# Attention's begin in a fused transformer kernel: sign rows by a copy, first stack from the projections, a store moved behind the max rows, fewer maxima in front

## The chip, the cores and the metric

The kernel is one program on 1 core of one Trainium2 chip. The metric is the device time in microseconds (us) of one execution. The times before are 1017.41, 1018.27 and 1013.22 us; the profiled execution is a further one.

## The reference, cut to what matters

Two macaron layers run over x, which has 1024 tokens of width 256. Each layer is half a feed-forward block, a mixing block, and half a feed-forward block again. The mixing block of the first layer is causal attention with 16 heads of width 16, and it is all that the change touches:

```
x = x + 0.5 * moe0(layernorm(x))
Q, K, V = (layernorm(x) @ W.T + b, split in 16 heads of 16)
scores = Q @ K.T / 4, causal mask          # 1024 x 1024 for each head
x = x + softmax(scores) @ V @ Wo.T + bo
x = x + 0.5 * moe0(layernorm(x))
...                                        # second layer: 8 experts, state-space mixer, 8 experts
```

## The kernel before

The kernel runs one queue of instructions on each engine, written out by hand; semaphores order them. PE is the matrix engine, DVE, ACT and POOL are the vector, scalar and GpSimd engines, SP only issues DMA copies. An engine does its instructions strictly in the order of the program.

**Attention's begin.** Behind the layernorm, PE makes eight projection groups (list `PROJ`: for each half e of the 256 output columns the matrix wk, then wq, each in two groups s of 512 tokens; L1241), each of 6 matmuls. ACT reads each group out of its PSUM bank as a rounded fp16 part (L1389), DVE subtracts that from the bank to get the small rest (L1431), so that q and k exist as a high and a low fp16 part. Two banks take turns. Then PE makes eight V tiles (L1251), and DVE adds their bias (L1438).

**Stacks.** The score products of a head want 3 x 16 rows of q and of k one above the other: high and low parts in the order of `ORDER`. SP stores the parts of q and k to DRAM (L1209, `wq_dram`, `wk_dram`, six copies for each half e, counted by `s_pd[e]`), and `stacks` (L1184) loads the 48 rows of a head from there. A pair of heads needs four such copies, q and k for two heads; they land in one of four slots, `qs[slot]` and `ks[slot]`. SP loads pair 0, ACT's queue pairs 1 and 2 and later, inside the loop, pairs 3 to 7.

**Maxima.** The softmax subtracts the row maximum of each query. For each pair, PE makes the scores once more in 12 pieces (`M_PIECES`; L1272, L1278) in two alternating pairs of banks, and DVE takes the maximum of each (L1454). Every fourth piece closes half s = 0 of a pair and every twelfth half s = 1; DVE then turns the columns (L1444) into `mt`. SP's `max_rows` stores `mt[s]` to `max_dram` (L1198), waits for its landing, and loads it as row 48 of `qs` for both heads (L1203). Opposite it in `ks` stands a row of -1 (`MAX_ROW`, written with its neighbours by DVE's memsets, L1425 and L1434), so that the matmul itself subtracts the maximum. The next pair's `mt[s]` waits until the store of this one's landed (`s_ms`).

**The loop.** The pairs' scores run in 8 x 5 = 40 steps g: scores (L1296, L1304), exponentials by ACT (L1408), the product with V (L1324) one step later, and the maxima of later pairs between them. `maxima_at(g)` says which pieces stand at which step: `M_LEAD = 9` steps ahead, so that 22 pieces (12 of pair 0, 10 of pair 1) stand ahead of step 0, and then 12 in each five steps (3, 2, 3, 2, 2, repeated). In front of the maxima PE runs 12 dummy matmuls, and 2 behind each piece (`keep_awake`, L114). The first score of a pair waits for its max rows (`s_mr`).

**Beside it.** `store_w1(2)` and `store_w1(3)` store the second half of a later layer's weights (4 copies of 1024 KB, L2308). They stand in SP's queue between the last store of q and k and the first `max_rows`. DVE waits for them only ahead of the next feed-forward block (`s_rows`). POOL splits other weights in 20 chunks, from the first score on (L1535 to L1548), and DVE's last additions of attention (L1519) wait for the last of these stores.

Of the kernel before, what the change touches and what calls it, by code (L numbers as in the profile page):

```python
# [10 lines left out]
F32 = mybir.dt.float32  # L11
F16 = mybir.dt.float16
# [25 lines left out]
NEG = -1e30  # L38
# [1032 lines left out]


def maxima_at(g):

    out, at = [], 0
    p, i = divmod(g + M_LEAD, NS)
    if 0 <= p < PAIRS:
        at = sum(M_STEPS[:i])
        out = [(p, n) for n in range(at, at + M_STEPS[i])]
    return out  # L1080

# [10 lines left out]
def attention_stage(c, src, A, region, mats, mats_ready, stage, stage_free, before_heads, store_w1):  # L1092
# [15 lines left out]
    w2l = region.take([2, W2_CHUNK], F16)  # L1108
    qs = region.take([STACKS - 1, T], F16)
    ks = region.take([STACKS - 1, T], F16)  # L1110
    spent = Region(region.tensor, region.size + 8 * D * KD)
    spent.at = region.size
    qs, ks = ([x[:, i, :] for i in range(STACKS - 1)] + [spent.take([T], F16)] for x in (qs, ks))
    at = region.at
# [25 lines left out]

    s_c = n("c", 16 * 4)
    s_m = n("m", 2)
    s_pj = n("pj", 8)
# [4 lines left out]
    s_va = n("va", NT)  # L1148
    s_ld = [c.sem(f"tile_in{i}", 16 * 4 * ((PAIRS + STACKS - 1 - i) // STACKS)) for i in range(STACKS)]
    s_sm = n("sm", PAIRS * NM)  # L1150
# [70 lines left out]

# [8 lines left out]
    def pe(eng):  # L1230
        L["pe"](eng)
        eng.wait_ge(*mats_ready)
        for j, (m, e, s) in enumerate(PROJ):
            eng.wait_ge(*L["lo"]((s + 1) * NT // 2 if m == "wk" else NT))
            if j >= 2:
                eng.wait_ge(*s_pl(j - 1))
            wh, wl = mats[m]
            i = 0
            for k in range(KD):
                for w, x in ((wh, c.XTh), (wl, c.XTh), (wh, c.XTl)):  # L1240
                    ins = eng.matmul(c.bank(j % 2), w[:, k, e * P:(e + 1) * P], tokens(m, x, k, s), start=(i == 0), stop=(i == 3 * KD - 1))  # L1241
                    i += 1
            ins.then_inc(s_pj.sem, 1)
        wh, wl = mats["wv"]
        for t in range(NT):
            if t >= 2:
                eng.wait_ge(*s_va(t - 1))
            i = 0
            for k in range(KD):
                for x, w in ((c.XTh, wh), (c.XTh, wl), (c.XTl, wh)):  # L1250
                    ins = eng.matmul(c.bank(2 + t % 2)[:, 0:D], x[:, k, t * P:(t + 1) * P], w[:, k, :],  # L1251
                                     start=(i == 0), stop=(i == 3 * KD - 1))
                    i += 1
            ins.then_inc(s_v.sem, 1)
# [5 lines left out]
        def maxima(p, n):  # L1260
# [3 lines left out]
            if n == 0:  # L1264
                eng.wait_ge(*s_ld[slot](64 * (p // STACKS + 1)))
            if i >= 2:
# [73 lines left out]

        for g in range(-M_LEAD, 0):
            for p, n in maxima_at(g):
                maxima(p, n)
                keep_awake(c, eng, 4, 2)
        for g in range(PAIRS * NS):
# [37 lines left out]
    def act(eng):  # L1383
        L["act"](eng)
        eng.wait_ge(*s_c(64))
        for j, (m, e, s) in enumerate(PROJ):
            eng.wait_ge(*s_pj(j + 1))
            b = 0 if m == "wq" else 1
            eng.activation(qk[m][0][:, e, s * BANK:(s + 1) * BANK], c.bank(j % 2), ACT.Identity, bias=bias[:, b, e:e + 1])\  # L1389
                .then_inc(s_ph.sem, 1)  # L1390

        eng.wait_ge(*s_pd[0](16 * 6))
        eng.wait_ge(*s_m(1))
        for p in range(1, STACKS - 1):
# [16 lines left out]

    def dve(eng):
        L["dve"](eng)
        link = c.dve_link
        eng.wait_ge(*s_c(64))
        eng.memset(zero32[:, :], 0.0)
        eng.memset(mh[:, :, :], 0.0)
        eng.tensor_copy(mask[:, 0:2, :], maskf[:, 0:2, :])
        eng.tensor_scalar(mask[:, 2:4, :], maskf[:, 2:4, :], NEG, None, ALU.mult)
# [7 lines left out]
        for j, (m, e, s) in enumerate(PROJ):  # L1427
            eng.wait_ge(*s_ph(j + 1))
            b = 0 if m == "wq" else 1
            tok = slice(s * BANK, (s + 1) * BANK)  # L1430
            eng.scalar_tensor_tensor(qk[m][1][:, e, tok], c.bank(j % 2), bias[:, b, e:e + 1], qk[m][0][:, e, tok],  # L1431
                                     ALU.add, ALU.subtract).then_inc(s_pl.sem, 1)
        for j in range(2):
            ins = eng.memset(ks[STACKS - 1][64 * j + 32:64 * j + 64, :], -1.0)  # L1434
        ins.then_inc(s_m.sem, 1)
        for t in range(NT):
            eng.wait_ge(*s_v(t + 1))
            eng.tensor_tensor(va[:, t, :, 0:DK], c.bank(2 + t % 2)[:, 0:D].rearrange("p (h v) -> p h v", v=DK),  # L1438
                              bv[:, :].rearrange("p (h v) -> p h v", v=DK), ALU.add).then_inc(s_va.sem, 1)
# [130 lines left out]
def attention_layouts(v):  # L1570
# [892 lines left out]
```

## Time and profile before

| what | before |
|---|---|
| median of three runs (lowest to highest) | 1017.41 us (1013.22 to 1018.27) |
| profiled execution, its own time | 1023.02 us |
| its span, first to last instruction | 1021.4 us |
| mean granted TensorE clock | 0.947 |
| PE, DVE, ACT, POOL busy | 858.3, 585.5, 395.8, 498.3 us |
| attention, first projection to last addition | 160.5 to 356.4 us |

Times in the rows are us from the span's start. A row of the timeline has its start, its length, engine and line, output and input; in square brackets stands how long the engine had been idle before it, and who ended that. "x6" is the number of instructions in the row. A q behind an engine's name (SPq, ACTq) is the engine's issue of a DMA copy. The chain of waits follows the work that ended last backwards, so that its rows are those that set the end.

### The profile page before, as it was taken

How to read it: one execution, taken by the hardware profiler on the slowest of the kernel's cores; microseconds unless marked ns; L12 is line 12 of the kernel's file. 1: busy time of each engine (PE TensorE's matmuls, PEld its weight loads, DVE VectorE, ACT ScalarE, POOL GpSimd, SP SyncE). 2: the span in 40 equal slices, each digit the busy share in tenths (PEclk: the TensorE clock that was granted, in tenths of full speed). 3: DMA queues.
4: the chain of work that ended last, by engine and by line, in shares of the span. 5: the costliest groups of instructions: out<-in, count | busy, mean ns of one | idle time of the engine just before them, and what ended most of it. 6: DMA issues, size and time to landing. Idle time of an engine off the chain costs nothing.

```text
span 1021.4 us, 21582 instructions
## 1 busy us (share of the span) xinstructions
PE 858.3 (84%) x7796; PEld 552.1 (54%) x7797; DVE 585.5 (57%) x1107; ACT 395.8 (39%) x957; POOL 498.3 (49%) x536
## 2 busy tenths in 40 slices
PE   3089986878877789998889999987889978999995
PEld 2046642323322344665578999634334444888994
DVE  5723345678988342334645555676699746544555
ACT  6322223126547442223244444277211152543441
POOL 2316758418888631212244554223988632544531
PEclk9999998999979978999799999999999998999998
DMA  8312654555555317202386665300000003675654
GB/s 295 113 37 93 206 182 139 181 187 180 180 178 158 117 54 290 92 22 69 113 323 230 247 218 207 99 1 1 0 1 1 0 32 136 222 246 180 220 182 140
DMA packets 47817, 142.25 MB, mean 139 GB/s; under 512 B 10641, under 2 KB 23778, under 8 KB 41218
## 3 DMA queue, kind: packets, MB, share of 16 engines
q0 software_dynamic: 19280, 93.40, 27.0%
q1 hardware_dynamic: 22430, 40.92, 11.4%
q10 hardware_dynamic: 6036, 6.95, 2.1%
q8 instruction: 50, 0.82, 0.3%
q14 instruction: 21, 0.17, 0.1%
HBM read 106.11 MB, written 35.16 MB: 138 GB/s over the span
## 4 chain that ended last, share of the span: by engine, by line
PE 56%; DVE 12%; DMA 9%; POOL 8%; issue 7%; ACT 7%; SPq 1%; another core or an unknown queue 0%; ACTq 0%; DVEq 0%; POOLq 0%
PE psum L570 15%; PE psum L543 10%; PE psum L529 10%; PE psum L1324 3%; DMA mem<-xn_dram,mem 2%; POOL mem L2133 2%; PE psum L114 2%; POOL mem L2129 2%; DMA wq_dram<-mem 2%; PE psum L554 2%; DMA max_dram<-mem 1%; PE psum L1296 1%; PE psum L516 1%; PE psum L1272 1%; DVE mem L1454 1%
## 5 line engine op out<-in xcount | busy, mean ns | idle before, releaser
L570 PE MATMUL psum<-mem 128*128 x1536 | 181.7, 274 | 7.1 <-issue 3.0
L570 PEld LDWEIGHTS psum<-mem 128*128 128x128 f16 x1536 | 146.3, 98 | 30.6 <-issue 11.3
L919 POOL DMA_INDIRECT y_dram<-mem x64 | 64.1, 1001 | 162.0 <-DVE mem L826 159.5
L661 ACT ACTIVATE mem<-psum,mem 128x128 f32<-128x128 f32 x368 | 104.7, 373 | 82.6 <-PE psum L543 42.9
L543 PE MATMUL psum<-mem 128*128 128x128 f16 x2208 | 132.3, 219 | 0.4 <-issue 0.2
L543 PEld LDWEIGHTS psum<-mem 128*128 128x128 f16 x2208 | 127.2, 98 | 2.1 <-issue 1.0
L914 POOL DMA_INDIRECT mem<-xn_dram,mem x64 | 67.0, 1048 | 108.1 <-PE psum L516 81.1
L1408 ACT ACTIVATE mem<-psum 128x512 f32<-128x512 f32 (+1 forms) x160 | 79.9, 552 | 76.3 <-PE psum L1304 53.3
L529 PE MATMUL psum<-mem 128*128 x432 | 103.0, 398 | 1.6 <-issue 1.6
L114 PE MATMUL psum<-ones 128*128 128x512 f16 x324 | 100.4, 435 | 0.6 <-issue 0.6
L1454 DVE TENSOR_REDUCE mem<-psum 128x2 f32<-128x1024 f32 (+2 forms) x96 | 87.8, 949 | 17.8 <-PE psum L1278 8.7
L817 DVE CAST mem<-mem 128x512 f16<-128x512 f32 x92 | 41.1, 446 | 98.3 <-ACT mem L661 89.7
L805 DVE TENSOR_TENSOR mem<-mem,psum 128x1024 f32<-128x1024 f32 x18 | 22.0, 1222 | 95.8 <-ACT mem L652 95.8
L529 PEld LDWEIGHTS psum<-mem 128*128 128x128 f16 x432 | 44.0, 102 | 54.2 <-issue 11.4
L895 POOL DMA_INDIRECT mem<-w_rows,mem x46 | 50.1, 1090 | 45.9 <-issue 24.7
L648 ACT ACTIVATE mem<-psum 128x256 f16<-128x256 f32 x64 | 24.8, 387 | 107.0 <-PE psum L516 104.8
L819 DVE TENSOR_TENSOR mem<-mem 128x512 f16<-128x512 f32 x92 | 64.3, 698 | 3.2
L1840 PE MATMUL psum<-mem 128*128 128x512 f32 x112 | 54.1, 607 | 10.9 <-DVE psum L2055 10.6
L196 PE MATMUL psum<-ident,mem 128*128 128x128 f32 x96 | 24.3, 341 | 35.1 <-ACT mem L180 35.0
L652 ACT ACTIVATE mem<-psum 128x1024 f32<-128x1024 f32 x18 | 18.4, 1024 | 88.4 <-PE psum L529 88.4
L516 PE MATMUL psum<-ident,mem 128*128 128x128 f32 x128 | 25.7, 284 | 31.2 <-DVE mem L315 14.1
L1324 PE MATMUL psum<-mem 128*17 128x384 f32 (+3 forms) x480 | 50.2, 453 | 0.7
(251 smaller groups left out, 1476.0 us busy)
## 6 DMA issues: line engine op xcount, KB each, us to landing
stage<-in_w POOLq DMA_DIRECT2D x20, 480.0 KB
stage<-in_w POOLq DMA_DIRECT2D x16, 512.0 KB
w_rows<-mem SPq DMA_DIRECT2D x8, 1024.0 KB, 8.4
w2h_dram<-mem POOLq DMA_DIRECT2D x20, 240.0 KB, 2.9
w2l_dram<-mem POOLq DMA_DIRECT2D x20, 240.0 KB, 3.4
xn_dram<-mem ACTq DMA_DIRECT2D x32, 128.0 KB, 1.7
mem<-w2h_dram SPq DMA_DIRECT2D x2, 2048.0 KB
mem<-w2l_dram SPq DMA_DIRECT2D x2, 2048.0 KB
```

The source lines that it names most:

```text
L114: eng.matmul(c.bank(bank), c.ones16[:, :], wide, start=True, stop=True)
L529: ins = eng.matmul(c.bank(2 * m + s), a[:, p, k, :], w[:, at], start=(i == 0), stop=(i == 3 * KD - 1))
L543: ins = eng.matmul(c.bank(2 * p + j // half)[:, j % half * P:(j % half + 1) * P], mats[q][:, l, k, j * P:(j + 1) * P], x[:, p, k, :], star ...
L570: ins = eng.matmul(c.bank(6)[:, 0:D], a[:, 0 if gated else p, q * half + j, :], w[:, at], start=(i == 0), stop=(i == 3 * CF - 1))
L661: ins = eng.activation(h[:, p, j * P:(j + 1) * P], c.banks(2 * p, 2)[:, j * P:(j + 1) * P], ACT.Gelu, bias=slabs[s][:, KD * FF + j:KD * FF ...
L819: eng.tensor_tensor(hTl[:, p, part, :], gelu, hTh[:, p, part, :], ALU.subtract).then_inc(s_hl.sem, 1)
L914: eng.indirect_dma_start(xg[:, b % 2, :], None, c.xn_dram[:, :], bass.IndirectOffsetOnAxis(ap=idx[:, b:b + 1], axis=0)).then_inc(s_xg[b % ...
L919: eng.indirect_dma_start(c.y_dram[:, :], bass.IndirectOffsetOnAxis(ap=yidx[:, b:b + 1], axis=0), yo[:, b % 2, :], None).then_inc(s_ys[b % ...
L1324: ins = eng.matmul(c.bank(7)[at:at + VW, a - y * BANK:a - y * BANK + w], va[:, k, 2 * p + j, :], pt[:, g % RING, 2 * y + j, off:off + w], ...
L1408: eng.activation(pt[:, g % RING, 2 * y + j, 0:w], c.bank(4 + at % 3)[:, 0:w], ACT.Exp, scale=DK ** -0.5).then_inc(s_ex.sem, 1)
L1454: eng.tensor_reduce(out, c.banks(2 * (i % 2), 2).rearrange("p (j q) -> p j q", j=2)[:, :, 0:w], AX.X, ALU.max)\
L1840: ins = eng.matmul(acc(2 * p + j), gm[:, i % RING, j, :], xw[:, i % RING, j, :], start=False, stop=True, skip_group_check=True)
```

## The change

- The row of -1 now comes by DMA from a constant in DRAM (`guard_rows`, `minus_ones`): two copies for slots 0 to 2 behind the other constants (the wait `s_c` of ACT, DVE and POOL includes them), two for slot 3 behind the stores of q and k. DVE's eight memsets go.
- Pair 0's stack no longer takes the way through DRAM: `first_stack` copies 16 rows at a time from the projections' SBUF tiles, 12 copies, nine issued by SP ahead of the stores, three by ACT ahead of its sixth group.
- The projections use four banks in turn, V's tiles banks 4 and 5.
- `store_w1(2)` and `store_w1(3)` stand behind the last `max_rows`.
- 16 pieces of maxima instead of 22 stand ahead of step 0 (`M_BEGIN`); each of steps 0 to 5 takes one more, from step 6 on all is as before.
- The wait for the mask and for all projections moves with these.

```diff
+M_BEGIN = 16
...
+def pieces_until(g):
+
+    if g < 0:
+        return M_BEGIN
+    p, i = divmod(g + M_LEAD, NS)
+    steady = NM * p + sum(M_STEPS[:i + 1]) if p < PAIRS else NM * PAIRS
+    ramp = M_BEGIN + sum(M_STEPS[(x + M_LEAD) % NS] + 1 for x in range(g + 1))
+    return min(steady, ramp)
...
 def maxima_at(g):
...
+    return [divmod(i, NM) for i in range(pieces_until(g - 1) if g >= 0 else 0, pieces_until(g))]
...
+    def first_stack(eng, m, j):
+
+        dst = (qs if m == "wq" else ks)[0]
+        for g, part_ in enumerate(ORDER[m]):
+            eng.dma_start(dst[64 * j + DK * g:64 * j + DK * (g + 1), :], qk[m][part_][j * DK:(j + 1) * DK, 0, :]).then_inc(s_ld[0].sem, 16)
+
+    def guard_rows(eng, i):
+
+        for j in range(2):
+            row = 64 * j + MAX_ROW
+            eng.dma_start(ks32[i][row:row + 1, :], A["minus_ones"][0:1, 0:ks32[i].shape[1]]).then_inc(s_c.sem, 16)
...
+        guard_rows(eng, 0)
...
+        eng.wait_ge(*s_pl(2))
+        for j in range(2):
+            first_stack(eng, "wk", j)
+        eng.wait_ge(*s_pl(4))
+        first_stack(eng, "wq", 0)
         for e in range(KD):
...
-            if e == 0:
-                eng.wait_ge(*s_pd[0](16 * 6))
-                eng.wait_ge(*s_m(1))
-                stacks(eng, 0)
+        guard_rows(eng, 1)
         eng.wait_ge(*s_pd[1](16 * 6))
-        store_w1(eng, 2)
-        store_w1(eng, 3)
         for p in range(PAIRS):
             for s in range(2):
                 max_rows(p, s)
+        store_w1(eng, 2)
+        store_w1(eng, 3)
...
-            if j >= 2:
-                eng.wait_ge(*s_pl(j - 1))
+            if j >= 4:
+                eng.wait_ge(*s_pl(j - 3))
...
+                if p == STACKS - 1:
+                    eng.wait_ge(*s_c(16 * 8))
...
-        eng.wait_ge(*s_c(64))
+        eng.wait_ge(*s_c(96))
         for j, (m, e, s) in enumerate(PROJ):
+            if j == 5:
+                eng.wait_ge(*s_pl(4))
+                first_stack(eng, "wq", 1)
             eng.wait_ge(*s_pj(j + 1))
...
-        for i in range(STACKS - 1):
-            for j in range(2):
-                ins = eng.memset(ks[i][64 * j + 32:64 * j + 64, :], -1.0)
-        ins.then_inc(s_m.sem, 1)
```

SP's queue from the projections to the first max rows, in the kernel before (`att_pl` counts DVE's rests of the projections, `att_pd1` the second half's stores, `att_mt` DVE's turned maxima):

```order
L1209 DMA wq_dram<-mem 128x1024 [waits att_pl]
L1209 DMA wq_dram<-mem 128x1024 x2
L1184 DMA mem<-wq_dram 48x1x1024 [waits att_m,att_pd0]
L1184 DMA mem<-wq_dram 48x1x1024
L1184 DMA mem<-wk_dram 48x1x1024 x2
...
L2308 DMA w_rows<-mem 128x2x1024 [waits split_lo,att_pd1]
L2308 DMA w_rows<-mem 128x2x1024
L2308 DMA w_rows<-mem 128x2x1024 [waits split_lo]
L2308 DMA w_rows<-mem 128x2x1024
L1198 DMA max_dram<-mem 4x32x32 [waits att_mt]
L1203 DMA mem<-max_dram 1x2x256 [waits att_ms0]
```

The same place of SP's queue in the changed kernel, from the constants on:

```order
L1211 DMA mem<-in_minus_ones 1x1536 x2
L1205 DMA mem<-mem 16x1024 [waits att_pl]
L1205 DMA mem<-mem 16x1024 x5
L1205 DMA mem<-mem 16x1024 [waits att_pl]
L1205 DMA mem<-mem 16x1024 x2
...
L1242 DMA wq_dram<-mem 128x1024 [waits att_pl]
L1242 DMA wq_dram<-mem 128x1024 x2
L1211 DMA mem<-in_minus_ones 1x512 x2
L1226 DMA max_dram<-mem 4x32x32 [waits att_mt,att_pd1]
L1231 DMA mem<-max_dram 1x2x256 [waits att_ms0]
L1231 DMA mem<-max_dram 1x2x256
```

The nine 16-row copies stand ahead of the twelve stores, the 48-row loads of pair 0 are gone from between them, and the first store of maxima has no weights' store in front.

DVE's queue from the constants to the first maxima, in the kernel before:

```order
L1422 MEMSET psum 128x512
L1425 MEMSET mem 32x1024 x6
L1431 SCALAR_TENSOR_TENSOR mem<-psum,mem 128x512 x8
L1434 MEMSET mem 32x1024 x2
L1438 TENSOR_TENSOR mem<-psum,mem 128x16x16 x8
L1454 TENSOR_REDUCE mem<-psum 128x2 x4
```

The same place in the changed kernel:

```order
L1454 MEMSET psum 128x512
L1455 CAST mem<-mem 128x256
L1456 TENSOR_SCALAR mem<-mem 128x256
L1461 SCALAR_TENSOR_TENSOR mem<-psum,mem 128x512 x8
L1465 TENSOR_TENSOR mem<-psum,mem 128x16x16 x8
L1481 TENSOR_REDUCE mem<-psum 128x2 x4
```

Six memsets in front of the first projection's rest and two in front of V's additions are gone; the two mask instructions, which stood ahead of the PSUM memset, now stand behind it.

## Rows read from the trace of the kernel before

**Rows 1.** Windows: us; PE, PEld, DVE, ACT, POOL busy; PEclk; DMA share; GB/s

```profile
162.00:170.00 8.00, 1.24 (x6) 0.39 (x4) 6.30 (x10) 1.37 (x2) 7.53 (x6) 0.91 0.45 132
182.00:205.00 23.00, 18.89 (x133) 8.93 (x130) 14.66 (x23) 1.97 (x2) 9.03 (x11) 0.93 0.46 173
205.00:222.00 17.00, 11.94 (x85) 3.54 (x84) 11.36 (x16) 0.25 (x1) 0.00 (x0) 0.90 0.51 195
222.00:240.00 18.00, 14.99 (x214) 6.00 (x214) 15.48 (x20) 14.07 (x28) 13.81 (x13) 1.00 0.54 166
```

**Rows 2.** Chain of waits, start and us: copies that set the end

```profile
178.19 3.27 DMA wq_dram<-mem
...
187.91 13.64 DMA wq_dram<-mem
...
204.93 9.91 DMA max_dram<-mem
...
275.58 5.24 DMA max_dram<-mem
...
281.43 5.83 DMA mem<-max_dram
```

**Rows 3.** Timeline of DVE, 163 to 215 us

```profile
163.15 0.91 DVE L1425 MEMSET mem<- 32x1024 f16 x1 [0.25 <-issue]
...
182.77 0.75 DVE L1431 SCALAR_TENSOR_TENSOR mem<-psum,mem 128x512 f16<-128x512 f32 x1 [1.06 <-ACT mem L1389]
...
195.42 0.43 DVE L1454 TENSOR_REDUCE mem<-psum 128x2 f16<-128x256 f32 x1 [3.14 <-PE psum L1278]
...
207.28 0.17 DVE L1461 TENSOR_TENSOR mem<-mem 128x8 f16<-128x8 f32 x1
...
214.94 0.21 DVE L1444 STREAM_TRANSPOSE mem<-mem 128x32 f16<-128x32 f16 x1 [4.15 <-DMA max_dram<-mem]
```

**Rows 4.** Timeline of PE, 160 to 222 us

```profile
160.48 0.59 PE L1241 MATMUL psum<-XTh,mem 128*128 128x512 f16 x2
...
170.80 1.01 PE L1241 MATMUL psum<-XTh,mem 128*128 128x512 f16 x2 [7.57 <-DVE mem L1431]
...
186.38 0.61 PE L1251 MATMUL psum<-mem,XTh 128*128 128x256 f16 x2 [3.05 <-DVE mem L1438]
...
192.38 2.75 PE L114 MATMUL psum<-ones 128*128 128x512 f16 x12 [0.56 <-issue]
...
221.24 0.39 PE L1296 MATMUL psum<-mem 49*128 49x512 f16 x2
```

**Rows 5.** Timeline of ACT: last projection, first copies of pair 2

```profile
182.05 0.69 ACT L1389 ACTIVATE mem<-psum,mem 128x512 f16<-128x512 f32 x1 [1.13 <-PE psum L1241]
...
185.61 1.41 ACTq L1184 DMA_DIRECT2D mem<-wq_dram  x2
```

**Rows 6.** Timeline of SP's issues, 201 to 220 us

```profile
201.57 3.31 SPq L2308 DMA_DIRECT2D w_rows<-mem  x4
...
216.11 0.56 SPq L1198 DMA_DIRECT2D max_dram<-mem  x1
218.08 1.15 SPq L1203 DMA_DIRECT2D mem<-max_dram  x2
```

**Rows 7.** Windows, same columns: the copies' tail, and the weights' store

```profile
199.00:200.00 1.00, 1.00 (x10) 0.29 (x8) 0.97 (x3) 0.00 (x0) 0.00 (x0) 1.00 0.20 78
207.00:210.00 3.00, 2.81 (x27) 1.00 (x26) 2.92 (x7) 0.00 (x0) 0.00 (x0) 1.00 1.03 408
```

**Rows 8.** Page, part 5: the maxima's reductions

```profile
L1454 DVE TENSOR_REDUCE mem<-psum 128x2 f32<-128x1024 f32 (+2 forms) x96 | 87.8, 949 | 17.8 <-PE psum L1278 8.7
```

**Rows 9.** Timelines of SP, POOL and DVE: attention's last rows

```profile
330.54 1.14 SPq L1203 DMA_DIRECT2D mem<-max_dram  x2
...
349.04 0.54 POOL L1548 DMA_DIRECT2D w2l_dram<-mem  x1
...
353.68 2.75 DVE L1519 TENSOR_TENSOR X<-psum,X 128x256 f32<-128x256 f32 x8 [0.64 <-PE psum L1337]
```

More of the change, by code:

```diff
@@ L1070, in unit_width @@
     return sum(query_span(k, y)[1] for k in S_KEYS[y][i])
-def maxima_at(g):
[L1075 to L1080, printed above, removed]
+def pieces_until(g):
[5 more added lines that the diff above has]
+    return min(steady, ramp)
+def maxima_at(g):
+    return [divmod(i, NM) for i in range(pieces_until(g - 1) if g >= 0 else 0, pieces_until(g))]
 def attention_weights(c, A, region):
@@ L1109, in attention_stage @@
     qs = region.take([STACKS - 1, T], F16)
+    at = region.at
+    ks32 = [region.take([(STACKS - 1) * T // 2], F32)]
+    region.at = at
     ks = region.take([STACKS - 1, T], F16)
@@ L1112, in attention_stage @@
     spent.at = region.size
-    qs, ks = ([x[:, i, :] for i in range(STACKS - 1)] + [spent.take([T], F16)] for x in (qs, ks))
+    qs = [qs[:, i, :] for i in range(STACKS - 1)] + [spent.take([T], F16)]
+    at = spent.at
+    ks32.append(spent.take([T // 2], F32))
+    spent.at = at
+    ks = [ks[:, i, :] for i in range(STACKS - 1)] + [spent.take([T], F16)]
     at = region.at
@@ L1139, in attention_stage @@
     CL = c.XTl[:, :, :].rearrange("p k t -> p (k t)").rearrange("p (g q) -> p g q", q=BANK)
-    s_c = n("c", 16 * 4)
-    s_m = n("m", 2)
+    s_c = n("c", 16 * 8)
+    s_m = n("m", 1)
     s_pj = n("pj", 8)
@@ L1148, in attention_stage @@
     s_va = n("va", NT)
-    s_ld = [c.sem(f"tile_in{i}", 16 * 4 * ((PAIRS + STACKS - 1 - i) // STACKS)) for i in range(STACKS)]
+    s_ld = [c.sem(f"tile_in{i}", 16 * 4 * ((PAIRS + STACKS - 1 - i) // STACKS) + (16 * 8 if i == 0 else 0)) for i in range(STACKS)]
+    stack_count = lambda p: 64 * (p // STACKS + 1) + (16 * 8 if p % STACKS == 0 else 0)
     s_sm = n("sm", PAIRS * NM)
@@ L1240, in pe @@
                 for w, x in ((wh, c.XTh), (wl, c.XTh), (wh, c.XTl)):
-                    ins = eng.matmul(c.bank(j % 2), w[:, k, e * P:(e + 1) * P], tokens(m, x, k, s), start=(i == 0), stop=(i == 3 * KD - 1))
+                    ins = eng.matmul(c.bank(j % 4), w[:, k, e * P:(e + 1) * P], tokens(m, x, k, s), start=(i == 0), stop=(i == 3 * KD - 1))
                     i += 1
@@ L1250, in pe @@
                 for x, w in ((c.XTh, wh), (c.XTh, wl), (c.XTl, wh)):
-                    ins = eng.matmul(c.bank(2 + t % 2)[:, 0:D], x[:, k, t * P:(t + 1) * P], w[:, k, :],
+                    ins = eng.matmul(c.bank(4 + t % 2)[:, 0:D], x[:, k, t * P:(t + 1) * P], w[:, k, :],
                                      start=(i == 0), stop=(i == 3 * KD - 1))
@@ L1264, in maxima @@
             if n == 0:
-                eng.wait_ge(*s_ld[slot](64 * (p // STACKS + 1)))
+                eng.wait_ge(*s_ld[slot](stack_count(p)))
             if i >= 2:
@@ L1339, in project @@
             return ins
[L1341 to L1344, printed above, removed]
+        for p, n in maxima_at(-1):
+            maxima(p, n)
+            keep_awake(c, eng, 4, 2)
         for g in range(PAIRS * NS):
@@ L1384, in act @@
         L["act"](eng)
-        eng.wait_ge(*s_c(64))
+        eng.wait_ge(*s_c(96))
         for j, (m, e, s) in enumerate(PROJ):
+            if j == 5:
+                eng.wait_ge(*s_pl(4))
+                first_stack(eng, "wq", 1)
             eng.wait_ge(*s_pj(j + 1))
             b = 0 if m == "wq" else 1
-            eng.activation(qk[m][0][:, e, s * BANK:(s + 1) * BANK], c.bank(j % 2), ACT.Identity, bias=bias[:, b, e:e + 1])\
+            eng.activation(qk[m][0][:, e, s * BANK:(s + 1) * BANK], c.bank(j % 4), ACT.Identity, bias=bias[:, b, e:e + 1])\
                 .then_inc(s_ph.sem, 1)
         eng.wait_ge(*s_pd[0](16 * 6))
-        eng.wait_ge(*s_m(1))
         for p in range(1, STACKS - 1):
@@ L1414, in dve @@
         link = c.dve_link
-        eng.wait_ge(*s_c(64))
+        eng.wait_ge(*s_c(96))
         eng.memset(zero32[:, :], 0.0)
         eng.memset(mh[:, :, :], 0.0)
-        eng.tensor_copy(mask[:, 0:2, :], maskf[:, 0:2, :])
-        eng.tensor_scalar(mask[:, 2:4, :], maskf[:, 2:4, :], NEG, None, ALU.mult)
         eng.memset(va[:, :, :, DK], 1.0)
@@ L1422, in dve @@
         eng.memset(c.bank(7), 0.0)
-        for i in range(STACKS - 1):
-            for j in range(2):
-                ins = eng.memset(ks[i][64 * j + 32:64 * j + 64, :], -1.0)
-        ins.then_inc(s_m.sem, 1)
-        for j, (m, e, s) in enumerate(PROJ):
-            eng.wait_ge(*s_ph(j + 1))
+        eng.tensor_copy(mask[:, 0:2, :], maskf[:, 0:2, :])
+        eng.tensor_scalar(mask[:, 2:4, :], maskf[:, 2:4, :], NEG, None, ALU.mult).then_inc(s_m.sem, 1)
+        for n, (m, e, s) in enumerate(PROJ):
+            eng.wait_ge(*s_ph(n + 1))
             b = 0 if m == "wq" else 1
             tok = slice(s * BANK, (s + 1) * BANK)
-            eng.scalar_tensor_tensor(qk[m][1][:, e, tok], c.bank(j % 2), bias[:, b, e:e + 1], qk[m][0][:, e, tok],
+            eng.scalar_tensor_tensor(qk[m][1][:, e, tok], c.bank(n % 4), bias[:, b, e:e + 1], qk[m][0][:, e, tok],
                                      ALU.add, ALU.subtract).then_inc(s_pl.sem, 1)
-        for j in range(2):
-            ins = eng.memset(ks[STACKS - 1][64 * j + 32:64 * j + 64, :], -1.0)
-        ins.then_inc(s_m.sem, 1)
         for t in range(NT):
             eng.wait_ge(*s_v(t + 1))
-            eng.tensor_tensor(va[:, t, :, 0:DK], c.bank(2 + t % 2)[:, 0:D].rearrange("p (h v) -> p h v", v=DK),
+            eng.tensor_tensor(va[:, t, :, 0:DK], c.bank(4 + t % 2)[:, 0:D].rearrange("p (h v) -> p h v", v=DK),
                               bv[:, :].rearrange("p (h v) -> p h v", v=DK), ALU.add).then_inc(s_va.sem, 1)
@@ L1490, in turn_back @@
                 eng.tensor_tensor(CL[:, g, :], cx[:, :], CH[:, g, :], ALU.subtract).then_inc(s_cl.sem, 1)
-        for g in range(-M_LEAD, 0):
-            for q, n in maxima_at(g):
-                maxima(q, n)
+        for q, n in maxima_at(-1):
+            maxima(q, n)
         for g in range(PAIRS * NS):
@@ L1524, in pool @@
         before_heads(eng)
-        eng.wait_ge(*s_c(64))
+        eng.wait_ge(*s_c(96))
         eng.wait_ge(*L["xn"](NT))
@@ L1584, in attention_layouts @@
     early = (m < 64) | (m - 64 < j)
+    d["minus_ones"] = np.full((1, 3 * T // 2), 0xBC00BC00, np.uint32).view(np.float32)
     d["causal"] = np.concatenate([m == j, m == j + 64, keys, early], 1).astype(np.float32)
```

2 lines of the change are left out of this document (1 added, 1 removed).

## The prediction, made before the changed kernel ran

> **What bounds the kernel now.** I read attention's begin first in the windows [rows 1]. Between 162 and 170 us PE is busy 1.24 of 8 us; between 205 and 222 it is busy 11.94 of 17 us, much of that with dummy matmuls, while ACT does next to nothing (0.25) and POOL nothing. From 222 on DVE is busy 15.48 of 18 us. So the begin is a chain of waits, and the loop behind it is nearly full on DVE. Then the timelines say what the chain is.
>
> PE starts the projections at 160.48 and stands still for 7.57 us, until DVE has done six memsets of 0.91 us and can free a bank [rows 3, 4]. DVE ends the last projection's rest at 182.77 + 0.75 = 183.5; two more memsets stand ahead of V's additions, and PE waits 3.05 us for those. At 192.38 the 12 dummies start, and DVE's first maximum comes at 195.42. Twelve maxima later, at 207.28 + 0.42 = 207.7, both halves of pair 0 are turned.
>
> SP is not ready for them. Its last store of the projections was issued at 187.91 and landed after 13.64 us, at 201.6 [rows 2]. In the tail of that landing the DMA engines show a share of 0.20 at 78 GB/s [rows 7]: about three of 16 engines work, and these carry the 48-row loads. Then SP issues 4 MB of weights (3.31 us, [rows 6]), which move at 408 GB/s, and the first store of maxima behind them takes 9.91 us, where the next one is landed and read from after 218.08 - 216.11 = 1.97 us. DVE meanwhile waits 4.15 us for the same landing. The first scores come at 221.24 [rows 4]. Everything behind them in attention is counted from there.
>
> **Memsets and banks.** The six memsets cost DVE 6 x (0.91 + 0.25) = 7.0 us ahead of its first rest. The mask instructions moved there are two short ones, and the two constant rows add two issues to SP; I allow 1 us for both, and take nothing: with four banks PE first looks for a rest at its fifth group, over 5 us after its start. So PE runs through. Twelve matmuls of 512 columns take 2.75 us at full clock [rows 4], so 48 take 11.0 and end at 160.5 + 11.0 = 171.5. ACT's extra work is three issues ahead of group six; one pair of its issues took 1.41 us [rows 5], so three take 2.1. The fourth rest is done at 160.5 + 5.5 + 0.69 + 0.75 = 167.4, ACT issues until 169.6 and has two groups to catch up, which it does at 0.69 each by 171.7. The last rest ends at 171.5 + 0.69 + 0.75 = 173.0, in place of 183.5.
>
> **V and first maxima.** From the last rest to the dummies it took 192.38 - 183.5 = 8.9 us. Two memsets with their gaps (2.3) go. PE's clock had fallen in the 3.05 us of idle time, and the two tiles after it took 188.91 - 186.38 = 2.5 us where tiles at full clock take 0.65 each; the new idle time is about 1 us, so 1.2 us more go. 173.0 + 5.4 = 178.4; the dummies and the first piece take the 195.42 - 192.38 = 3.0 us that they took. First maximum at 181.4, which is 14.0 us earlier.
>
> **Pair 0's stack.** It must be there at 181.1. SP can issue its first copy at 160.5 + 2.8 + 1.4 = 164.7 and nine by 171 at up to 0.7 each; some 8 us are left behind the last one, so this is hidden if 16 rows move as a store does. What that is, no row shows. From above, the nearest row is the 48-row load: 96 KB by three engines [rows 7], 25 GB/s for each. Were a 16-row copy on a single engine, 12 x 32 KB would take 15.5 us from 165.5 on, and with that engine's part of the stores (6 x 16 KB, 3.9 us) end at 181 to 185. From below: spread over all engines it is under 1 us each. I take the lower one: the 48 rows are read as three blocks of 16 in DRAM and three engines work, so the outer count, not the rows, seems to set the number; a 16-row copy has no outer count but its rows. The Trainium skill says the same (DMA: Bandwidth & Descriptors, Queues, rings and completion order): a copy uses the largest number up to 16 that divides the slowest dimension on both sides, so 3 for the load and 16 for the copy. By that rule the sum has nothing here, by one engine up to 4 us; the trace agrees on the 3. The same rule speaks against the next step, for the store of maxima has 4 as slowest dimension and shares its engines with the loads of pairs 1 and 2.
>
> **Projections' stores and max rows.** SP issues the twelve stores behind its nine copies, from 171 to 177, the last one after 173.0. The first six land some 3.3 us after the last of them [rows 2], at 177 or 178, and ACT then issues eight loads of 96 KB. At 78 GB/s these keep their engines for 10 us; the second six stores' share there is 3.9 us more. All have landed by 192 at the latest, probably 184 for the stores. The maxima of pair 0 are turned at 181.4 + 12.3 = 193.7. So the stores aren't the last wait any more; at worst the first half's store starts at 192 and delays the second by 1 us. From 193.7 on: store 1.97, two loads' issues 1.15 [rows 6], and their landing, which took at most 221.24 - 219.23 = 2.0. First scores at 198.8, **22.4 us earlier**. PE has its 16 pieces done at about 181.4 + 15.4 = 197 and waits some 2 us. Pair 1's stack is issued first of the eight and wanted at 194; it is there.
>
> **Fewer maxima in front.** Six reductions of 949 ns [rows 8] come into steps 0 to 5, 5.7 us on the engine that was busy 15.48 of 18 us [rows 1]. The gaps that it had, 2.5 us, can hide some. Between 3 and 5.7, I take 5: PE's pieces wait for DVE one by one, so few gaps close. Counted on DVE alone it comes out near: 14.0 earlier at the first maximum, 4.15 of wait and 1.4 of slow clock behind it gone, 3.5 of new wait at the first score, 16.1. By the scores it is 22.4 - 5 = 17.4. I take **17**.
>
> **The store behind.** The last max rows are read at 330.54 + 1.14 = 331.7 [rows 9], now 314.7. 4 MB alone take 10 us at 408 GB/s [rows 7]; beside POOL's chunks (166 GB/s, [rows 1]) some 16, so it lands by 331 to 334. DVE wants it at 356.4 - 17 = 339. POOL's chunks start with the first score and ended at 349.6, 127 us later; now at 326 or, slowed by the store, 330, and attention's last addition wants them at 336.7. Both are hidden by 5 us. The 2 constant rows of slot 3 are hidden by three pairs of steps.
>
> **Rivals.** (1) *The sixteen-row copies are slow*, by one engine as above, or the second stores' landing is later than 192. First maxima up to 4 us later, first scores 3 to 5 later: gain 12 to 14. (2) *The ramp costs more*: pair 1's maxima are complete in step 2 and wanted in step 5, three steps after, where it was five. At the worst seen round trip, 5.24 + 1.15 + 5.83 = 12.2 us [rows 2, 6], that is late by about 2 us beyond 10 us of steps; with DVE's 5.7 the gain is 22.4 - 8 = 14, together with (1) 10. (3) *No change*: the front was not what set the end of attention, POOL's 20 chunks were: they ended at 349.6, just 4 us before the last addition. Against it: they start with the first score, so they move too. Only if the weights' store stretched them by more than the 7 us that they now have, and by 12 more, nothing would be left. (4) *Slower*: the weights' store behind the max rows holds up the next block. It decides when it lands after 356, that is 41 us after its issue, at under 100 GB/s. Rows 7 show four times that, but no row shows it beside the loop's end. At 80 GB/s it would land at 367 and the kernel take 1028 us.
>
> **How the numbers follow.** The profiled execution took 1023.0 us, 5.6 above the median of 1017.4. The sum makes 1006.0 of the first, and **1000.4** of the median. The forecast with its own bounds, 14 to 22 less (all of the six maxima hidden at the one end), has a chance of 0.77; rivals 1 and 2, 8 to 14 less, 0.15; rival 3, within 0.5%, 0.05; rival 4, 0.03. What this kernel can tell from no change is about 0.5%, or 5 us. Range: 1017.4 - 22 = 995 less 1 for the spread of runs, and 1017.4 - 10 = 1007.4: 994 to 1007.5. Faster 0.92, same 0.05, slower 0.03.
>
> **What would show it.** Right: PE's projections without a gap and at full clock, the last rest near 173, first maximum near 181, first scores near 199, their max rows as the last wait; DVE's share up between 199 and 220; last addition near 337 with PE as its releaser. Wrong: an idle PE for the first piece with the 16-row copies as releaser (rival 1); a wait of the scores at step 5 (rival 2); a wait of DVE between attention's last addition and the next layernorm (rival 4); the last addition released by POOL's stores (rival 3). The step most open is what the six maxima cost.

## The result, and the profile after

The changed kernel takes 1007.69 us (median of 20 runs), the kernel before 1017.54 (20 runs): ratio 0.9903, 95% interval 0.9885 to 0.9921. It is faster by 9.85 us, where 17 were predicted; the time lies just outside the range of 994 to 1007.5.

The profiled execution of the changed kernel took 1007.78 us, its span is 1005.9. Its windows, from the first score to 211 us, from there to pair 0's context, and from there to pair 1's (columns as in [rows 1], to be held against the last row there):

```profile
199.14:211.00 11.86, 10.26 (x70) 3.12 (x72) 6.61 (x7) 5.43 (x10) 7.11 (x8) 0.50 0.40 130
211.00:223.91 12.91, 9.84 (x144) 4.04 (x140) 11.39 (x14) 6.31 (x14) 11.63 (x11) 0.97 0.61 185
223.91:244.06 20.15, 15.82 (x190) 5.91 (x192) 16.77 (x20) 10.23 (x21) 17.56 (x17) 0.83 0.59 182
```

PE runs at half clock for the first 12 us of the loop, and pair 0's context (its product with V, turned by DVE) comes 24.8 us after the first score. In the kernel before that took 15.8 (237.0 - 221.24). What lies ahead of the loop came as forecast. The timeline of DVE:

```profile
162.25 0.75 DVE L1461 SCALAR_TENSOR_TENSOR mem<-psum,mem 128x512 f16<-128x512 f32 x1 [0.63 <-ACT mem L1423]
...
171.25 0.75 DVE L1461 SCALAR_TENSOR_TENSOR mem<-psum,mem 128x512 f16<-128x512 f32 x1 [0.17 <-ACT mem L1423]
...
180.18 0.43 DVE L1481 TENSOR_REDUCE mem<-psum 128x2 f16<-128x256 f32 x1 [3.14 <-PE psum L1308]
...
192.05 0.27 DVE L1488 TENSOR_TENSOR mem<-mem 128x8 f16<-128x8 f32 x1
...
223.91 0.71 DVE L1500 STREAM_TRANSPOSE mem<-psum 128x512 f32<-128x512 f32 x1
```

The last rest ends at 172.0 (173.0 predicted, 183.5 before), the first maximum comes at 180.2 (181.4; 195.4 before), both halves of pair 0 are turned at 192.6 (193.7; 207.7 before) [rows 3]. The timeline of PE:

```profile
159.97 0.59 PE L1271 MATMUL psum<-XTh,mem 128*128 128x512 f16 x2
...
172.40 0.39 PE L1281 MATMUL psum<-mem,XTh 128*128 128x256 f16 x2 [0.59 <-DVE mem L1465]
...
177.14 2.75 PE L114 MATMUL psum<-ones 128*128 128x512 f16 x12 [0.56 <-issue]
...
199.14 0.61 PE L1328 MATMUL psum<-mem 49*128 49x512 f16 x2 [4.30 <-DMA mem<-max_dram]
...
208.02 0.61 PE L1302 MATMUL psum<-mem 48*128 48x512 f16 x2 [0.84 <-DVE mem L1481]
...
221.61 0.39 PE L1328 MATMUL psum<-mem 49*128 49x512 f16 x2 [0.47 <-DMA mem<-max_dram]
```

The projections run through, the idle time of 7.57 us is gone and that of 3.05 is 0.59 [rows 4]; the first scores come at 199.1 (198.8 predicted). But behind the 4.30 us of idle time ahead of them the clock is half, and at 221.61 step 5 waits for max rows again, 0.47 us. SP's issues:

```profile
164.26 5.63 SPq L1205 DMA_DIRECT2D mem<-mem  x9
169.94 1.58 SPq L1242 DMA_DIRECT2D wk_dram<-mem  x3
...
186.01 0.62 SPq L1226 DMA_DIRECT2D max_dram<-mem  x1
193.53 1.20 SPq L1231 DMA_DIRECT2D mem<-max_dram  x2
194.76 0.56 SPq L1226 DMA_DIRECT2D max_dram<-mem  x1
...
214.62 0.54 SPq L1226 DMA_DIRECT2D max_dram<-mem  x1
217.46 1.13 SPq L1231 DMA_DIRECT2D mem<-max_dram  x2
```

The nine 16-row copies are issued by 169.9, and no wait names them. Pair 1's second half is turned only at 214.6 and its rows are wanted at step 5: the chain of waits, from there on.

```profile
186.01 7.50 DMA max_dram<-mem
...
194.76 2.03 DMA max_dram<-mem
...
214.62 2.82 DMA max_dram<-mem
...
218.05 3.51 DMA mem<-max_dram
...
221.61 0.39 PE psum L1328 x2
```

In this pair of profiles attention ends only 5.2 us earlier (356.4 to 351.3). A second pair, e17 and e18 below, shows 10.2 us (360.6 to 350.4), and no gain in what lies behind attention.

### The profile page after: what moved, and what is told of

It reads as the page before. It is cut to its first block, busy times and chain, and to the rows that moved or that the text cites. A ratio compares the mean times of both kernels' runs of the same rounds, so it can differ in the third digit from the quotient of the medians.

```text
span 1005.9 us, 21558 instructions
## 1 busy us (share of the span) xinstructions
PE 856.9 (85%) x7784; PEld 553.7 (55%) x7785; DVE 591.5 (59%) x1099; ACT 398.4 (40%) x957; POOL 490.9 (49%) x536
## 4 chain that ended last, share of the span: by engine, by line
PE 61%; DVE 11%; DMA 7%; ACT 7%; POOL 7%; issue 6%; SPq 1%; ACTq 0%; DVEq 0%; POOLq 0%
PE psum L570 16%; PE psum L543 12%; PE psum L529 10%; PE psum L1356 3%; PE psum L114 2%; POOL mem L2160 2%; DMA max_dram<-mem 2%; DVE mem L1481 2%; PE psum L554 2%; PE psum L516 2%; POOL mem L2156 1%; PE psum L1328 1%; ACT mem L180 1%; PE psum L1923 1%; DVE mem L315 1%
## 5 line engine op out<-in xcount | busy, mean ns | idle before, releaser
L570 PE MATMUL psum<-mem 128*128 x1536 | 178.8, 273 | 3.7 <-DVE mem L810 2.5
L529 PE MATMUL psum<-mem 128*128 x432 | 99.3, 388 | 1.6 <-issue 1.6
L817 DVE CAST mem<-mem 128x512 f16<-128x512 f32 x92 | 45.0, 489 | 78.1 <-ACT mem L661 77.0
L895 POOL DMA_INDIRECT mem<-w_rows,mem x46 | 45.4, 986 | 44.9 <-issue 27.1
L1356 PE MATMUL psum<-mem 128*17 128x384 f32 (+3 forms) x480 | 54.3, 490 | 0.5
```

Of the source, the lines that this page charges most:

```text
L529: ins = eng.matmul(c.bank(2 * m + s), a[:, p, k, :], w[:, at], start=(i == 0), stop=(i == 3 * KD - 1))
L570: ins = eng.matmul(c.bank(6)[:, 0:D], a[:, 0 if gated else p, q * half + j, :], w[:, at], start=(i == 0), stop=(i == 3 * CF - 1))
L1356: ins = eng.matmul(c.bank(7)[at:at + VW, a - y * BANK:a - y * BANK + w], va[:, k, 2 * p + j, :], pt[:, g % RING, 2 * y + j, off:off + w], ...
```

## The experiments

Four to a chip, except the last two. A ratio is to the kernel before on the same chip, with its 95% interval. Each profile is of one execution. "Pair 0" is the time from the first score to the first context turned (row 128x512 of DVE, L1473 before, L1500 after).

**e1, 16 dummies over the wait; e2, 22 maxima in front.**

```diff
# e1, behind the loop over maxima_at(-1)
+        keep_awake(c, eng, 4, 16)
# e2
-M_BEGIN = 16
+M_BEGIN = 22
```

> The changed kernel with 16 more dummy matmuls (about 3.6 us) behind the 16 maxima in front, over the wait for the first max rows; nothing else. Theory A (the idle 4.3 us before the first scores drop PE's clock, and the ramp, which has no dummies, then runs some 13 us at half clock): first scores stay at 199, the granted clock of the first pair's steps rises from 0.75 to over 0.95, and the first pair's steps take 20 us or less in place of 24.8; ratio to before about 0.986. Theory B (the five more maxima on DVE are the whole cost): the clock rises but the first pair's steps stay at 24 us; ratio stays 0.990.

> The changed kernel with 22 maxima in front, as before the change (M_BEGIN = 22), all other edits kept. Theory A and the lead: six more pieces with their dummies fill the wait, first scores at 201 to 203, the first pair's steps take 16 us as in the kernel before, pair 1's max rows are no longer waited for at step 5; ratio 0.983 to 0.986. Rival (fewer maxima in front is a gain, as the scores start earlier): slower than the changed kernel, ratio 0.992.

e1: 999.93 us, 0.982 (0.9774 to 0.9865). e2: 997.79 us, 0.980 (0.9758 to 0.9842). In the profile of e1, the slowest of its six runs, 1.44 us of idle time are left and the clock falls all the same: pair 0 took 24.5 us. In e2 the first scores come at 201.6 without any wait and pair 0 takes 15.8 us, as before the change. Fewer maxima in front were no gain but a loss. e2's end shows what the weights' store does there, in the timeline of DVE:

```profile
337.13 2.74 DVE L1545 TENSOR_TENSOR X<-psum,X 128x256 f32<-128x256 f32 x8 [2.09 <-DMA w2l_dram<-mem]
```

The last additions wait 2.1 us for POOL's last store. In its repetition e15 the same row waits 0.64 us, for PE.

**e3, weights' store back in front; e4, behind the max rows of pair 1.**

```diff
# e3: ahead of the loop over p; e4: in it, if p == 1
+        store_w1(eng, 2)
+        store_w1(eng, 3)
```

> The changed kernel with the 4 MB weights' store back ahead of the first max rows. If the store's place is worth what the sum says, the first scores come 8 to 10 us later (at 207 to 209) and the ratio is 0.996 to 1.000. Rival (the store behind costs at the end what it gives in front, since the last pair's steps took 1.6 us longer and the loop is bound by DVE): first scores later, but the ratio stays within 0.002 of 0.990.

> The changed kernel with the weights' store behind the max rows of pair 1 in place of behind the last ones. If the store behind slows the last pairs (the last pair took 16.1 us for 14.4), this gives back about 1.5 us at the end but costs the max rows of pair 2, whose lead of five steps should hide it: ratio 0.988 to 0.990. If the end's 1.6 us are only PE's clock, no difference: 0.990.

e3: 1015.05 us, 0.9984 (0.9946 to 1.0022), first scores at 212.9 behind 16.5 us of idle PE. The store's place is worth 14 us at the first score and nearly the whole gain. e4: 1019.05 us, 1.0026 (1.0 to 1.0052), my figure of 0.988 to 0.990 missed. The chain of waits of e4:

```profile
223.74 20.88 DMA max_dram<-mem
```

One max store takes 20.9 us to land behind the 4 MB in its queue, beyond the lead of a pair: pair 1's steps took 30 us.

**e5, 19 in front; e6, a busy PE in the ramp; e7, pair 0's stack through DRAM; e8, the store issued by ACT.**

```diff
# e5
+M_BEGIN = 19
# e6: 20 dummies behind the front, and in maxima, ahead of the piece
+            if 16 <= i < 36:
+                keep_awake(c, eng, 2 * (i % 2), 2)
# e7 (M_BEGIN = 22): no first_stack; in sync, behind the stores of e == 0
+                eng.wait_ge(*s_pd[0](16 * 6))
+                stacks(eng, 0)
# e8 (M_BEGIN = 22): in act, none in sync
+            if g in (24, 31):
+                store_w1(eng, 2 if g == 24 else 3)
```

> The changed kernel with 19 maxima in front (M_BEGIN = 19), between its 16 and the 22 that gave 0.980. Theory A (what counts is that PE is kept busy over the wait for the first max rows, and that pair 1's maxima end early enough): PE has its pieces done at about the time the max rows land (199.5), no idle time there, and most of the gain is there: ratio 0.981 to 0.984. Theory B (each piece that stays in the steps costs its 0.95 us on DVE and more by what waits on it, whatever the clock): half way, 0.985.

> The changed kernel (16 maxima in front) with 20 dummy matmuls over the wait for the first max rows and two dummies ahead of each of the next 20 pieces of maxima, in the bank that the piece then overwrites; no arithmetic of the kernel is changed. Theory A (the granted clock in the first pairs' steps is the loss): clock of the first pair's steps over 0.9, its 24.8 us fall to 20, ratio 0.980 to 0.983, as 0.4 us of dummies per piece partly replace what the clock gives. Theory B (DVE's five more pieces and the pair 1 max rows' lead): the clock rises, the first pair's steps stay at 23 us or more, ratio 0.987 or above.

> The kernel with 22 maxima in front (0.980), and pair 0's stack again loaded from DRAM behind the first half's stores, in place of the twelve 16-row copies. The sum gave the 16-row copies no cost and their gain only as cover: the stack landed at 181.5 + before; with the projections 10 us earlier it would land at about 182 to 183, some 3 us after the dummies end at 179.8, and the second half's stores and the first max rows come later by the 5 us of the four loads on three engines. Expected first scores at 204 to 206 in place of 201.6, ratio 0.983 to 0.985. Rival (the way through DRAM is hidden behind V's products): 0.980.

> The kernel with 22 maxima in front (0.980), and the weights' store issued by ACT's queue in two halves, ahead of its exponentials of steps 24 and 31, in place of by SP behind the last max rows. With 22 in front the last additions waited 2.1 us for POOL's last store and the block behind them for more, as the 4 MB ran at 382 GB/s beside POOL's last chunks. If that contention is the wait, it goes: attention ends 2 to 3 us earlier, ratio 0.977. Rival (the halves slow the max rows of the last pairs instead, as the store in the middle of SP's queue did with 20.9 us): 0.980 or above.

On this chip the runs spread widely (before: 1021 to 1036). e5: 1012.91 us, 0.983 (0.9774 to 0.9885). That is in theory A's range, but the interval holds B's 0.985 too, and the profile, of the slowest of its six runs, does not look as A said: 1.74 us of idle time are left, the clock falls to 0.50 from 203 on, and pair 0 takes 21.4 us. So it does not decide.

e6: 1019.39 us, 0.9932 (0.9896 to 0.9969): its clock is 1.00, and pair 0 takes 26.3 us. By the letter that is theory B, but the dummies are up to 0.44 us per piece on a PE that is now busy 25.1 of these 26.3 us, DVE 17.2. It takes the clock out and puts as much in, so it separates nothing.

e7: 1024.35 us, 0.9925 (0.9884 to 0.9966): the timeline of PE.

```profile
191.06 0.29 PE L1300 MATMUL psum<-mem 48*128 48x128 f16 x2 [10.03 <-DMA mem<-wk_dram]
```

Ten us of wait for the stack, where I had put 3; the direct copies are worth 12 us at the first score (213.8 against 201.6).

e8: 1012.4 us, 0.9841 (0.9788 to 0.9895): no wait for POOL at the end, but 4.1 us for max rows in the last pairs, as the rival said.

**e9, 24 dummies; e10, the store in four pieces; e11, 22 with the store in front; e12, short reductions.**

```diff
# e9
+        keep_awake(c, eng, 4, 24)
# e10 (M_BEGIN = 22): in max_rows' loop, one copy a pair
+            if p >= PAIRS - 4:
+                store_w1(eng, 2 + (p - PAIRS + 4) // 2, (p - PAIRS + 4) % 2)
# e12: the reduction's columns
+[:, :, 0:w if i < 16 or i >= 33 else 64]
```

> The changed kernel (16 maxima in front) with 24 dummies (5.3 us) over the wait for the first max rows, so that no idle time is left ahead of the first scores; none in the steps. With 16 dummies 1.4 us of idle time was left, and in its profile the clock still fell to half at 201. Theory A (idle time ahead of and in the first steps drops the clock, which costs about 5 us there): clock of the first pair's steps 0.95 or more, its 24.8 us fall to 19 to 20, ratio 0.980 to 0.983. Rival C (the short waits inside the first steps drop the clock whatever comes before): the clock falls again at 202, steps 24 us, ratio 0.985 to 0.990.

> 22 maxima in front, and the weights' store cut in its four copies of 1 MB, one in SP's queue behind the max rows of each of pairs 4 to 7. Each holds up the next max rows by 1 MB, 2.5 us alone and about 5 beside POOL's chunks (4 MB took 20.9). The lead of the max rows is a pair, 17 us, and their trip 11: if that holds, no score waits, and the end's wait for POOL's last store (2 to 3 us) goes: 3 us less than with 22 in front and the store behind. Rival: the trip grows beyond the lead as with ACT's issue (4.1 us of wait for max rows), no gain or a loss of 2 to 4 us.

> 22 maxima in front, and the weights' store back ahead of the first max rows: sign rows by copy, four banks and the direct stack alone against the kernel before. With 16 in front that was 0.998, with 16.5 us of idle PE ahead of the first scores at 212.9. With 22 in front the scores come no earlier (212 to 213), but six pieces are done in that wait: 5 to 6 us less than with 16, ratio 0.992. Rival (DVE's wait for the landing of the first store of maxima blocks these six): 0.998.

> The changed kernel, but the maxima that stand in steps 0 to 5 are taken over only 64 columns per head, so that part of the maximum is left out; DVE's time for these 17 falls from about 16 to 5 us. Theory B (the first pair's steps are bound by DVE's five more maxima): the steps take 17 us or less, ratio 0.982 or below. Theory A (PE at half clock is the bound there, DVE waits for it 13 of 25 us): the steps keep 22 us or more, ratio 0.987 to 0.990.

e9: 1008.23 us, 0.9823 (0.9785 to 0.9861). e12, whose kernel leaves out part of the maximum, is no version to use: 1007.22 us, 0.9807 (0.9761 to 0.9852). Both split what I had held for one cause. The windows of e9 (clock kept) and then of e12 (DVE freed), up to pair 0's context:

```profile
199.77:216.00 16.23, 12.51 (x181) 5.12 (x180) 13.46 (x18) 9.65 (x20) 11.60 (x12) 1.00 0.45 147
216.00:223.41 7.41, 3.75 (x34) 1.10 (x32) 3.32 (x4) 1.88 (x5) 6.51 (x7) 0.84 0.60 191
```

```profile
199.39:211.00 11.61, 11.04 (x104) 3.95 (x106) 2.85 (x11) 6.15 (x12) 6.59 (x8) 0.60 0.36 122
211.00:223.68 12.68, 8.86 (x112) 3.08 (x110) 3.31 (x12) 5.40 (x12) 11.40 (x11) 0.81 0.59 186
```

With full clock up to 216 or with an almost free DVE, the context comes at 223.4 and 223.7, as in the changed kernel. In both the score of step 5 waits over 3 us; the timeline of PE in e9:

```profile
220.50 0.39 PE L1328 MATMUL psum<-mem 49*128 49x512 f16 x2 [3.33 <-DMA mem<-max_dram]
```

Pair 1's second half is turned at 210.0, its store lands after 6.0 us, the second load is issued 0.6 us later and lands after 3.8: a trip of 10.5 us. That was rival 2 of the prediction. The gain of both over the changed kernel comes later: pairs 1 to 4 take 71 us in each in place of 75, and from pair 4's context to attention's end it is 46.9 and 47.0 us in place of 52.1. Attention ends at 341.3 and 341.7, ten us before the changed kernel.

e10: 1008.94 us, 0.9838 (0.9788 to 0.9889), waits of 2.0 us for max rows and 1.2 for a stack in the later pairs, no gain over the store behind. e11: 1014.58 us, 0.9878 (0.9828 to 0.9927), with first scores at 214.4; my 0.992 lies in the interval, the rival's 0.998 does not.

**e13, POOL's chunks later; e14, the changed kernel; e15, e2 again; e16, memsets and two banks.**

```diff
# e13, with e9's dummies, in pool
-        eng.wait_ge(*s_st(1))
+        eng.wait_ge(*s_st(4 * NS + 1))
# e16 (M_BEGIN = 22), c.bank(j % 2), and in dve ahead of the first rest
+        for i in range(STACKS - 1):
+            for j in range(2):
+                eng.memset(ks[i][64 * j + 32:64 * j + 64, :], -1.0)
```

> The changed kernel with the 24 dummies over the wait (as e9), and POOL's chunks begun with step 5's first score in place of step 0's, so that pair 1's max rows travel without them. Theory L (pair 1's max rows, turned 10 us after the first score, take a 10.5 us trip because POOL's chunks share the DMA engines, and step 5 waits for them): the trip from the turned maxima to the score falls to 5 to 7 us, no wait at step 5, pair 0's context is turned 19 to 20 us after the first score in place of 23.6. Rival (the trip is long by the loads of pair 3 on ACT's queue alone): the trip stays at 9 to 10 us, and so does the wait. The total says nothing here, as POOL's chunks then end some 15 us after attention's last product.

> The changed kernel as it is, on the same chip as the next run. The interval of 0.9885 to 0.9921 should hold it: 0.990. First scores at 199, pair 0's context 23 to 25 us later, with half clock or with a wait at step 5.

> The kernel with 22 maxima in front once more, beside the changed kernel on one chip. If its 0.980 was no accident of that chip: 0.978 to 0.983, and 7 to 10 us below the changed kernel. If the difference was the chip's: within 3 us of it.

> 22 maxima in front, and the memsets of slots 0 to 2 back ahead of the first rest, with two banks in turn in place of four; all other edits kept. The sum's term for memsets and banks was 10.5 us at the last rest. Expected: last rest near 182 in place of 172, first scores at 209 to 212 in place of 201.6, ratio 0.988 to 0.991. Rival (the copies of the stack and of the projections were the longer way to the first scores, so memsets cost less): first scores at 206 or earlier, ratio 0.984.

e13, one execution: 1008.04 us. The rows of pair 1 are turned at 209.7 and the score at 216.70 waits for nothing; the context comes at 219.0, 19.5 us after the first score. SP's issues in e13, to be held against those above:

```profile
209.72 0.54 SPq L1226 DMA_DIRECT2D max_dram<-mem  x1
213.16 1.13 SPq L1231 DMA_DIRECT2D mem<-max_dram  x2
```

The store is back after 3.4 us in place of 6.0.

e14: 1005.97 us, 0.9872 (0.9828 to 0.9916). e15: 996.33 us, 0.9813 (0.9783 to 0.9843): 9.6 us below it on one chip, attention's end at 340.2 against 349.1. But e15 is e2's kernel, and its pair 0 took 17.3 us where e2's took 15.8. Its windows, up to pair 0's context and to pair 1's:

```profile
200.56:217.89 17.33, 15.41 (x201) 5.96 (x202) 13.31 (x17) 11.96 (x24) 12.39 (x13) 0.90 0.47 155
217.89:232.87 14.98, 12.63 (x184) 5.00 (x182) 13.43 (x20) 9.99 (x21) 13.17 (x12) 1.00 0.64 200
```

The clock fell to 0.67 between 206 and 209 although nothing waited ahead of the first score, so one execution's clock is no constant of a kernel.

e16: 1005.79 us, 0.9893 (0.9864 to 0.9923): last rest at 184.7, first scores at 213.2. The memsets and banks are worth 12 us there (201.6 in e2, 200.6 in e15).

**e17, the kernel before; e18, the changed kernel,** each as it is, one round.

> The kernel before, as it is, for a second profile beside one of the changed kernel on the same chip. In the first profiles attention ended 5.2 us earlier (356.3 against 351.2), but the spans differed by 15.5, so that 10 us lay behind attention, where no instruction was changed, while the medians differ by 9.85. If that was chance of one execution: attention ends near 356, and from there to the end of the span it takes 655 to 660 us in place of 665. If what lies behind attention gains by the change (the weights' store or POOL's chunks elsewhere): 665 again, and 10 more than in the run beside it.

> The changed kernel on the same chip as the run before this one. From attention's end to the end of the span 654 to 656 us, as in its two profiles so far (654.7, 654.8); attention's end at 349 to 351, if the kernel before has 356 on this chip.

e17: 1014.27 us (one of its eight runs took 1706 us, for no reason that the record shows), 0.9964 (0.9936 to 0.9992) against the same kernel, so that a difference of 0.4% in one round means nothing. e18: 1002.93 us, 0.9866 (0.9729 to 1.0004). Attention ends at 360.6 and 350.4; from there to the span's end it is 655.4 and 656.1. The first profile of before had 665 there, which this one does not repeat.

## Why the prediction was wrong

**The front was right.** Memsets and banks: last rest 11.5 us earlier, 10.5 predicted; e16 puts them at 12. V and first maximum: 15.2 earlier, 14.0 predicted. Pair 0's stack cost nothing, and e7 shows what it saved. By the rule of the Trainium skill (DMA: Bandwidth & Descriptors, Why a DMA increments its semaphore by 16 and not by 1) a 16-row copy works on 16 engines; the trace agrees in so far as twelve copies were there in time, their spread itself is in no row. Projections' stores: max rows of pair 0 started at 186.0 and not at 192; but their store took 7.50 us beside the loads of pairs 1 and 2 (DMA share 0.20 at 74 GB/s from 186 to 193.5), so the second half began 2.2 us after it was turned, where 1 was priced; the first maximum's head start paid for it. First scores 22.1 us earlier in the first profiles, 22.4 predicted, and 24.9 in e17 and e18.

**The step that failed is "Fewer maxima in front".** I took 5 us of 3 to 5.7, counting only six reductions on DVE. The first pair's steps alone grew by 9.0 us (24.8 against 15.8; 25.1 against 15.8 in e18 and e17), and on one chip 16 pieces in front (e14) cost 9.6 us against 22 (e15) in the kernel's time. The runs divide the 9.0 us: 3.8 us are the five pieces themselves (e13: 19.5 us with clock and rows in order). 4.1 us more come from pair 1's max rows (e9: 23.6). With half clock in place of that it is 1.1 more (24.8). Clock and rows overlap: in the changed kernel the maxima are turned at 214.6 in place of 210, and the trip then takes 7 us in place of 10.5, the store 2.8 us in place of 6.0. Of the 4.6 us later 1.3 are in DVE's small maximum of 128x8 (L1488) just before: it takes 1.46 us in place of 0.17, and ends with POOL's instruction beside it (214.35 and 214.33). The rest goes with the half clock. Either way the score of step 5 comes at 220 or 221.6. Rival 2 had this mechanism, at 2 us; I put the steps between at 10 us and the trip at 12.2, but even in e13 only 7.0 us lie between the turned rows and step 5's score, as the rows are turned 10 us after the first score.

**The clock was no term at all.** I saw the wait of 2 us coming (it was 4.30, as PE had its pieces done at 194.8) and gave it no price by the clock. In the kernel before, the pieces behind the 4.62 us of idle time ahead of 216.32 carried two dummies each. Windows of the kernel before:

```profile
216.00:219.00 3.00, 2.68 (x12) 0.65 (x12) 2.40 (x4) 0.00 (x0) 0.00 (x0) 0.55 0.06 9
219.00:222.00 3.00, 2.93 (x21) 0.79 (x20) 2.19 (x4) 0.25 (x1) 0.00 (x0) 0.88 0.03 3
```

The clock was back at 1.00 from 222 on [rows 1]. Now the loop's own steps follow the idle time, and they have no dummies. It stays half for 12 us. That the dummies make this difference is argued: no run has them in the steps alone. Behind that, pair 1's steps have a clock of 0.83 and take 20.2 us, before 0.90 and 17.9. Pairs 1 to 4 took 75.2 us in place of 71.4: about 4 us of loss behind the ramp, which nothing in the prediction foresaw. A full clock in the ramp (e9) or a shorter DVE there (e12) each bring 71 back. The clock within these pairs is not what differs: its mean is 0.86 in the changed kernel, 0.87 in e9 and 0.88 before, and e9's pair 1 takes 17.6 us at 0.78. What the ramp leaves behind that costs these 4 us stays open.

**The store behind** was right in front, where e3 and e11 show 13 to 14 us at the first score. From pair 4's context to attention's end the changed kernel takes 52.1 us in place of 48.0 (50.9 against 49.0 in e18 and e17). The record does not lay that on the store. 2.5 us of the 4.1 are pair 5's steps (299.13 to 317.66), and SP issues the store only at 325.3. Windows of the changed kernel and of e9:

```profile
299.13:317.66 18.53, 15.18 (x184) 5.79 (x182) 14.67 (x20) 10.00 (x21) 16.04 (x16) 0.82 0.52 161
```

```profile
294.47:309.37 14.90, 12.63 (x184) 5.04 (x182) 13.35 (x20) 10.00 (x21) 12.82 (x11) 1.00 0.49 158
```

The other 1.6 are the last pair, 16.1 us at a clock of 0.89 for 14.5 at 1.00, which the kernel before shows too (e17: 15.9 at 0.89). e9 and e12 have the same store behind and take 46.9 and 47.0 us; e3 has it in front and takes 49.8. So this loss goes with the clock; why that is lower there stays open. What the store does cost at the end shows with 22 in front: POOL's last load took 10.1 us in e2, and the last additions waited 2.1 us. Sum for the second pair of profiles: 24.9 - 9.4 - 3.4 - 1.9 = 10.2, which is the measured gain of attention; for the first pair it is 22.1 - 9.0 - 3.8 - 4.1 = 5.2.

**How many maxima stand in front** therefore decides about half of it: with 22 the same edits give 20.5 and 18.0 us (0.9813 and 0.980), about twice the changed kernel's. But the number itself is not the only way: e1 and e9 keep 16 in front, only fill the wait with dummies, and stand at 0.982 with overlapping intervals, although e9's first pair still takes 23.6 us. So most of what e9 wins back (10 us at attention's end) does not come from the first pair's steps.

## What to carry to other kernels

Work that fills a wait is free only while the wait is there, and it may also be what keeps PE's clock up and a later transfer in time; before moving it out, look at what then stands behind the idle time, and price the steps after it too. Count a lead in microseconds from the instruction that completes the data to the one that wants it, with the worst trip seen, and not in steps. A large store ahead of small urgent copies in one queue holds them all up (14 us at the first score here); behind them it was cheap, and in the middle no better than in front (1.003 and 0.998).

## What the runs showed of the hardware

- After 4.30 us of idle PE the granted clock was 0.50 for 12 us, though PE was busy 10.3 of 11.9 us; after 1.44 us (e1) it fell too, within 2 us, in steps with short waits. With none ahead of the first score it stayed 1.00 in e2, and in e9 up to 221, but in e15, e2's kernel again, it was 0.76 from 203 to 206 and 0.67 to 209.
- A small store behind the 4 MB store in its queue landed after 9.91 us in front of the loop [rows 2], and after 20.9 us beside POOL's chunks (e4).
- The first store of maxima took 7.50 us while eight 48-row loads were under way, and the next one 2.03 us. In the ramp one took 6.0 us beside POOL's chunks (e9) and 3.4 without them (e13).
- DVE's small maximum of 128x8 took 1.38 to 1.54 us where a POOL instruction ran beside it (the changed kernel, e1, e14, e18), and 0.17 us in e9, e12 and e13.
